# Ternary weights prepared beside the expert tiles, and attention rows gathered behind a batch's parts

## What is computed

```python
# layer 1 ffn: 8 experts, 2 for each token
topk_logits, selected = jax.lax.top_k(hidden_states @ Wr, 2)
p = jax.nn.softmax(topk_logits)
for e in range(8):
    w_e = jnp.where(selected == e, p, 0.0).sum(-1, keepdims=True)
    g = jnp.clip(silu(x @ Wg[e]), -7.0, 7.0)
    out = out + ((g * (x @ Wu[e])) @ Wd[e]) * w_e
# layer 2 attention: 8 heads a batch, 16 rows of 128 to a head
sm = softmax(einsum('bdm,bdn->bmn', qh, kh) * scale);  ret = einsum('bmn,bcn->bcm', sm, vh)
# layer 2 ffn: three matrices, each rounded to -1, 0, 1 by the mean of its absolute values
s = 1.0 / clip(mean(abs(w)), 1e-5);  qw = clip(round(w * s), -1, 1) / s
# layer 3 attention (16 heads a batch, masked), layer 3 ffn: three matrices, rounded the same way
q = clip(round(w / mean(abs(w))), -1, 1) * mean(abs(w))
```

## Time and profile before

| | us |
|---|---|
| median of the 3 runs (2516.19 to 2522.55) | 2522.51 |
| the profiled execution | 2525.09 |
| its span, first to last instruction | 2523.3 |
| MoeTop2 (1451.8 to 1629.5), its tile loop from about 1506 | 177.7 |
| Attention 2 (1629.6 to about 1843) | 213 |
| Attention 3 (2058 to about 2386) | 328 |

### The profile page before, as it was taken

How to read it: one execution, slowest core, us unless ns; L and a number is a source line. 1 busy time by engine, 2 the same in 40 slices (tenths; PEclk the granted TensorE clock), 3 DMA queues, 4 the chain that set the end, 5 groups by cost and what they waited for, 6 DMA issues and landing times. The chain is left out here.

```text
span 2523.3 us, 42640 instructions
## 1 busy us (share of the span) xinstructions
PE 2034.0 (81%) x13467; PEld 1242.7 (49%) x13467; DVE 1814.2 (72%) x4020; ACT 1403.7 (56%) x3553; POOL 1186.2 (47%) x1393
## 2 busy tenths in 40 slices
PE   5999698996799999999999849837835437887487
PEld 2444265663567776777777646514412223333144
DVE  4899485665799999999998663368837756888254
ACT  0777422451688888888888713215634423677343
POOL 3444102443788888888887523276312204333100
PEclk9999779998999999999999959958866656899699
DMA  4466313782300000000000042379610025576100
GB/s 133 138 188 171 100 48 106 249 260 82 59 16 20 20 22 16 20 20 22 16 16 3 1 151 88 117 188 237 174 47 1 0 87 133 153 198 159 44 1 34
DMA packets 256886, 223.20 MB, mean 88 GB/s; under 512 B 36441, under 2 KB 237756, under 8 KB 256028
## 3 DMA queue, kind: packets, MB, share of 16 engines
q1 hardware_dynamic: 231932, 173.06, 24.3%
q0 software_dynamic: 12240, 32.39, 5.1%
q10 hardware_dynamic: 12496, 15.03, 1.8%
HBM read 141.98 MB, written 79.32 MB: 88 GB/s over the span
## 5 line engine op out<-in xcount | busy, mean ns | idle before, releaser
L844 ACT ACTIVATE a_PT<-bank 128x512 f32<-128x512 f32 x640 | 355.8, 602 | 148.7 <-PE bank L607 132.3
L734 DVE TENSOR_REDUCE a_nm<-bank 128x2 f32<-128x512 f32 x640 | 409.2, 683 | 35.1 <-PE bank L600 32.9
L600 PE MATMUL bank<-a_stack_k,a_stack_q 48*128 48x256 bf16 (+2 forms) x1280 | 263.2, 298 | 108.9 <-DVE a_nm L734 75.3
L2913 PE MATMUL bank<-f_w,f_zc 128*128 128x512 bf16 x1152 | 283.9, 383 | 22.8 <-DVE f_zc L3021 18.2
L3233 POOL TENSOR_TENSOR f_hr<-f_hr,half_pow 128x4 f32<-128x4 f32 x192 | 244.5, 1273 | 84.8 <-DVE f_hr L3030 84.6
L607 PE MATMUL bank<-a_stack_q,a_stack_k 51*128 51x256 bf16 (+2 forms) x1280 | 252.2, 287 | 8.6 <-ACT a_PT L844 8.0
L600 PEld LDWEIGHTS bank<-a_stack_k,a_stack_q 48*128 48x128 bf16 (+2 forms) x1280 | 91.7, 99 | 272.9 <-DVE a_nm L734 195.8
L3125 ACT ACTIVATE f_Pm<-bank,f_nmax 128x128 f32<-128x128 f32 x512 | 182.5, 382 | 73.5 <-DVE f_nmax L3045 73.5
L622 PE MATMUL bank<-a_PT,a_V 128*32 128x256 f32 x2560 | 188.3, 416 | 1.4 <-ACT a_PT L844 1.4
L2913 PEld LDWEIGHTS bank<-f_w,f_zc 128*128 128x128 bf16 x1152 | 112.2, 99 | 123.0 <-issue 25.4
L3222 POOL TENSOR_TENSOR f_cf<-f_cbr,f_cmr 128x516 f32<-128x516 bf16 x128 | 157.0, 1226 | 12.6 <-DVE f_cb L3070 11.0
(11 more groups left out here) (370 smaller groups left out, 4721.2 us busy)
## 6 DMA issues: line engine op xcount, KB each, us to landing
cut<-a_parts SPq DMA_DIRECT2D x96, 192.0 KB
cut<-a_parts SPq DMA_DIRECT2D x144, 128.0 KB
o<-a_O SPq DMA_DIRECT2D x32, 512.0 KB
a_stack_q<-cut SPq DMA_DIRECT2D x64, 192.0 KB
a_stack_k<-cut SPq DMA_DIRECT2D x64, 192.0 KB
m_w<-in_w SPq DMA_DIRECT2D x32, 368.0 KB
moe_out<-m_oe ACTq DMA_DIRECT2D x32, 256.0 KB
a_num<-o SPq DMA_DIRECT2D x48, 128.0 KB
```

Of the source, the lines that this page charges most:

```text
L600: x = t.matmul(ps[:, n * D:(n + 1) * D], self.stack_q[rows, i, slot, n * P:(n + 1) * P], self.stack_k[rows, i, slot, :], start=True, stop= ...
L734: v.tensor_reduce(self.nm[:, g % 2, :, at % self.J, at // self.J], self.k.bank[h % 3][:, :].rearrange("p (n m) -> p n m", n=2), AX.X, ALU. ...
L844: a.activation(self.PT[:, h % 8, :, :].rearrange("p m n -> p (m n)"), self.k.bank[3 + h % 3][:, :], ACT.Exp).then_inc(self.a_exp.sem, 1)
L2913: x = t.matmul(ps[:, :], self.zc[:, b % 2, j, c_, :], self.fp8.w3[:, m, c_, at:at + BANK], start=(m == 0 and c_ == 0), stop=(m == 2 and c_ ...
```

## The change

1. The ternary weights of both layers leave the attentions. `MoeTop2` gets both `TernaryWeights`; the float copies and sums are allocated in its memory, the rounded bf16 matrices and the means in memory that lasts to the end. SP loads the matrices in 15 pieces of at most 768 columns (9 for layer 2, 6 for layer 3): six ahead of the first tile's store, three ahead of each of the next three stores. DVE sums in the tile steps 4 to 12, one piece behind `product` and one behind `copy_out`; PE adds over the partitions at step 13; DVE rounds from step 14 on, two instructions a step.
2. `pairs.gather(b + 2)` moves on POOL from offset 0 of batch b to its offset 15.
3. The eight PSUM banks become slices of one tensor; `two_banks` isn't called.

The core of the diff:

```diff
 class TernaryWeights:
     def allocate(self, ctx):
-        self.w = s("wf", [P, 3, self.width])
-        self.w16 = s("w16", [P, 3, self.width], BF16)
+        self.w16, self.m = s("w16", [P, 3, self.width], BF16), s("m", [P, 3])
+    def allocate_work(self, ctx):
+        self.w = s("wf", [P, 3, self.width])
-    def load(self, e):
+    def loads(self, e):
         for j, n in enumerate(self.names):
-            e.dma_start(self.w[:, j, :], self.k.A[n]).then_inc(self.d_w.sem, 16)
+            for at, size in self.pieces:
+                e.dma_start(self.w[:, j, at:at + size], self.k.A[n][:, at:at + size]).then_inc(self.d_w[j].sem, 16)
+                yield
 class Attention(Stage):
     def dve(self, v):
-            if 0 <= t < 60:
-                next(sums, None)
...
-            if t > 61:
-                next(steps, None)
     def act(self, a):
-        if self.ternary:
-            self.ternary.load(a)
     def pool(self, g):
                 if at < self.NV:
                     self.clear_V(g, at)
-                if self.pairs and at + 2 < B:
-                    self.pairs.gather(g, at + 2)
...
                 g.tensor_tensor(self.parts[:, i, :, 2, :], self.rest[:, i, :, :], self.parts[:, i, :, 1, :],
                                 ALU.subtract).then_inc(self.g_p2.sem, 1)
+            at = self.starts(t, 15)
+            if at is not None and self.pairs and at + 2 < B:
+                self.pairs.gather(g, at + 2)
 class MoeTop2(Stage):
+    TOTAL = 13
     def sp(self, sp):
         self.load_experts(sp, range(4, self.NE))
+        weights = chain.from_iterable(x.loads(sp) for x in self.ternaries)
         for j in range(self.NT):
+            for _ in range(3 if j else 6):
+                next(weights, None)
             sp.wait_ge(self.v_oe.sem, self.v_oe.at(j + 1))
     def pe(self, t):
+            if i == self.TOTAL + 2:
+                for x in self.ternaries:
+                    t.wait_ge(x.v_mean.sem, x.v_mean.at(1))
+            if i == self.TOTAL:
+                t.wait_ge(self.a_xT.sem, self.a_xT.at(i - 1))
+                for n, x in enumerate(self.ternaries):
+                    x.total(t, self.at_total(n))
     def dve(self, v):
                 self.product(v, i - 1)
+            if 4 <= i < self.TOTAL:
+                next(sums, None)
+            if i > self.TOTAL:
+                next(rounding, None)
             if i >= 3:
                 self.copy_out(v, i - 3)
+            if 4 <= i < self.TOTAL:
+                next(sums, None)
+            if i == self.TOTAL:
+                v.wait_ge(self.p_xT.sem, self.p_xT.at(i + 1))
+                for n, x in enumerate(self.ternaries):
+                    x.means(v, self.at_total(n))
+            if i > self.TOTAL:
+                next(rounding, None)
```

More of the change, by code:

```diff
@@ L1 @@
 from contextlib import ExitStack
+from itertools import chain
 import numpy as np
@@ L102, in __init__ @@
         self.sig = Signals(nc, ctx)
-        self.bank = [ctx.enter_context(nc.psum_tensor(f"bank{i}", [P, BANK], F32)) for i in range(8)]
+        self.psum = ctx.enter_context(nc.psum_tensor("bank", [P, 8 * BANK], F32))
+        self.bank = [self.psum[:, i * BANK:(i + 1) * BANK] for i in range(8)]
         self.X = self.sb("X", [P, B, D])
@@ L674, in dve @@
         self.dve_parameters(v)
-        sums = self.ternary.sums(v) if self.ternary else iter(())
-        steps = self.ternary.rounding(v) if self.ternary else iter(())
         for t in self.steps():
@@ L1982, in dve @@
         self.list_tokens(v)
+        sums = chain.from_iterable(x.sums(v) for x in self.ternaries)
+        rounding = chain.from_iterable(x.rounding(v) for x in self.ternaries)
         for i in range(self.NT + 3):
@@ L1989, in dve @@
                 self.places(v)
+            if 4 <= i < self.TOTAL:
[6 more added lines that the diff above has]
+                next(rounding, None)
+        for _ in rounding:
+            pass
     def moments(self, v, g):
@@ L3249, in program @@
         if 0 in stages:
-            stage(Attention(k, 0, None))
+            stage(Attention(k, 0))
         if 1 in stages:
@@ L3258, in program @@
         with ExitStack() as memory:
-            pairs = Pairs(k) if 3 in stages else None
-            if 3 in stages:
-                pairs.allocate(memory)
-                stage(MoeTop2(k, pairs))
+            pairs = Pairs(k)
+            l2.allocate(memory)
+            l3.allocate(memory)
+            with ExitStack() as rows:
+                pairs.allocate(rows)
+                if 3 in stages:
+                    stage(MoeTop2(k, pairs, (l2, l3)))
+                if 4 in stages:
+                    stage(Attention(k, 2, pairs))
             if 4 in stages:
-                l2.allocate(memory)
-                stage(Attention(k, 2, l2, pairs))
                 stage(Bitnet(k, l2))
-        if 6 in stages:
-            with ExitStack() as memory:
-                l3.allocate(memory)
-                stage(Attention(k, 3, l3))
+            if 6 in stages:
+                stage(Attention(k, 3))
                 stage(TernaryFfn(k, l3))
```

48 lines of the change are left out of this document (21 added, 27 removed).

## The result

The changed kernel takes 2600.6 us (median of 4, 2596.4 to 2603.6) against 2522.1 us before (2516.2 to 2522.6): 1.0316 times as long, interval 1.0292 to 1.0339, or +78.5 us. The forecast of 2601 us holds.

A forecast was written before the change was run, and what follows sets the result against it. No single engine was taken to bound the kernel; each stage has its own limit. Terms +93.8 - 5 - 11 + 1 = +78.8 us on 2525.1 gave 2603.9, stated as 2601 us against the runs' median, range 2562 to 2630.

The forecast's parts named there:

- The ring: Attention 2: moving the gather closes a loop of parts, gather, landing, add, moments and ACT's first part; +93.8 us.
- landing, among heads: Attention 2, later batches: time from the gather's second issue until its rows land, taken as 5.2 us, ends 2.8 and 6.6.
- moments to parts: fill, middle, heads: Attention 2: from DVE's moments to the end of ACT's first part, 2.3 us early, 4 between, 6.6 later with hand-over.
- rival 1: Attention 2: every gather lands in the shortest 2.8 us, turns of 12.0, 13.8 and 16.3 us; 2572 us, chance 0.22.
- The start: Attention 2: without 3 MB of weight loads batch 0's rows land sooner, so the chain starts 3.9 us earlier (0 to 3.9).
- MoeTop2: Tile loop taking over the weights' sums and roundings: PE could stall 0 to 3 us, taken as +1; no gain possible.
- Rival 4: MoeTop2's loop gives the gain back, costing +5 to +8 us instead of +1; 2607 us, sharing the forecast's chance of 0.54.
- Layer 3: Attention 3 without weights: 9.1 us of rounding and 2 us of sums go, -11 us (-9 to -14).
- The tail of Attention 2: Layer 2: ten rounding instructions behind batch 15's add go, 0.5 us each, -5 us (-2 to -7).
- PE's clock: Attention 2: pauses put PE at 1.2 GHz part of the time, granted clock nearer 0.6 than 0.71; link 6.5 us.
- 2 had 14.8, 17.6 and 20.7: Rival with a slower loop in Attention 2: landings 5.6 and 6.6 us, PE's clock low throughout; 2627 us, chance 0.16.
- Rival 3: Faster than before: the gather's wait in Attention 2 is hidden and the weights' move gains; 2493 us, chance 0.06.

The follow-up runs named there:

- The dose of 1.9 us a turn: Changed kernel with two of POOL's three instructions for the parts done twice in layer 2: 2631.1 us, 1.0431 of the kernel before.

## Why the prediction was right, point by point

**What waits for what** held, and it is what carried the forecast. The ring was put together from the order of the lists and from single links of the trace of before, and all of its links are in the trace of after, with nothing else between them. The two halves separately, +99.5 us on the adds for the gather and 31 us less time for the weights, settle it against the weights' move. The gather at the same place with one batch more of lead, 100 us faster, settles it against the place in POOL's list. The dose of 1.9 us a turn that came back 14 times shows that the turn is the sum of its links.

**The links**, as predicted and as measured in the changed kernel:

| link | predicted us | measured us |
|---|---|---|
| parts to second issue | 5.0 | 4.6; 5.3 in the last three turns |
| landing, fill | 4.3 | 4.6 to 5.4, mean 4.95 (batches 3 to 6) |
| landing, among heads | 5.2 | 3.7 to 5.3, mean 4.6 |
| add and moments | 1.9 | 1.87 |
| moments to parts: fill, middle, heads | 2.3, 4, 6.6 | 2.4, 3.8, 6.4 to 6.85 |
| four turns in the fill | 54 | 55.3 |
| two in the middle | 32.4 | 30.2 |
| seven among heads | 130.9 | 126.4 |

From the first issue (1635.08) to add 15 the changed kernel needs 231.9 us where 238.1 were predicted: 6 too many, most of it the landing among heads. The reason given for taking 5.2, traffic as before plus SP's stores of the same parts, left out that a ring at half the pace has less traffic (DMA share 0.54 against 0.92 in the earlier trace rows). How much each of the two does to the landing no run separates. All landings of the gathers in the ring, from a query of their line between 1640 and 1870 us; it counts both DMAs of a pair, each from its own issue, where the table counts from the second issue to the add:

```profile
DMA to landing us min/median/max: 3.1/3.7/5.4
```

None is as short as rival 1 wanted throughout (2.8 us; two turns with 2.9 were seen in the kernel with the gather ahead of the parts). The term for parts to second issue was too long by 0.4 us in eleven turns. The estimate of 2.3 us by the Trainium skill ("DMA: Bandwidth & Descriptors", "Anatomy of one DMA") is under every landing measured here; the measurement decides. A link wasn't in the forecast: POOL's addition into X, 0.7 us, which from batch 13 on stands between parts and gather.

**The start.** First issue to first add 7.94 us before, 4.10 after: 3.84 sooner, as the 3.9 predicted. The stage itself began 3.4 us later, so add 0 stands where it stood. That the weights' loads were the reason is borne out by the kernel with the gather alone, which still has them: 8.26 us.

**MoeTop2**, predicted +1. DVE's timeline in a turn with two sums:

```profile
1522.96 0.29 DVE L2179 TENSOR_SCALAR n_sg<-n_sg 128x256 f32<-128x256 f32 x1 [1.87 <-ACT n_sg L2232]
...
1523.70 0.95 DVE L263 TENSOR_REDUCE w_gate_sums<-w_gate_wf 128x1 f32<-128x768 f32 x1
...
1524.89 0.94 DVE L263 TENSOR_REDUCE w_gate_sums<-w_gate_wf 128x1 f32<-128x768 f32 x1
1525.98 0.29 DVE L2179 TENSOR_SCALAR n_sg<-n_sg 128x256 f32<-128x256 f32 x1
```

The turn stays at 3.02 us and the idle time of 1.87 us is used up. (A sum takes 0.86 us here; the rows that the prediction cites give 0.85, which changes nothing.) PE is busy for all of 18 us and all of 40 us in two windows of the loop at granted clock 1.00, and its two matmuls with the totals cost some 0.4 us. The stage began 1.9 us later than in the trace of before and ended 3.4 later; the difference, 1.5, is near the 1 predicted, and 1.1 of it lies ahead of the first tile, where none of this work is. From the loop's first clamp to its last it is 112.8 and 112.7 us in the two kernels with the weights in the attentions and 113.2 to 113.6 in the ten traces with them here: the loop pays 0.4 to 0.9 us. Rival 4 (the loop gives the gain back) isn't seen.

**Layer 3**, predicted -11: from Bitnet's first moments to TernaryFfn's 498.1 us, before 510.2: -12.1. SP's first store of each batch's parts in Attention 3 tells where. In the kernel before, the batches 2 to 4:

```profile
2104.03 0.38 SPq L520 DMA_DIRECT2D cut<-a_parts  x1
2124.94 0.38 SPq L520 DMA_DIRECT2D cut<-a_parts  x1
2141.52 0.41 SPq L520 DMA_DIRECT2D cut<-a_parts  x1
```

and in the changed kernel the batches 2 to 7:

```profile
2193.63 0.38 SPq L526 DMA_DIRECT2D cut<-a_parts  x1
2210.20 0.39 SPq L526 DMA_DIRECT2D cut<-a_parts  x1
2227.01 0.41 SPq L526 DMA_DIRECT2D cut<-a_parts  x1
2241.07 0.41 SPq L526 DMA_DIRECT2D cut<-a_parts  x1
2256.03 0.51 SPq L526 DMA_DIRECT2D cut<-a_parts  x1
2270.57 0.51 SPq L526 DMA_DIRECT2D cut<-a_parts  x1
```

The turns of 19.7 and 18.0 us, to the batches 6 and 7, are now 15.0 and 14.5: -8.2 where -9.1 was put. The turn to batch 3, behind the six sums, fell from 20.9 to 16.6: -4.3 where -2 was put, inside its bounds of 0 and 5.2. So the term is there with both its parts. "14.3 us a batch through" was too smooth all the same: the turns to the batches 3 and 4 take 16.6 and 16.8 us with nothing rounded beside them, and the second took 16.6 before.

**The tail of Attention 2**, predicted -5 for ten roundings behind add 15: add 15 to Bitnet's first moments took 86.8 us before and 85.4 after, -1.4. This term failed in size. The ten roundings are there behind the add of batch 15, and they cost what was put, but only for a while: the ninth maximum behind that add comes 13.0 us after it before and 11.6 with the gather alone, against 7.9 to 10.2 in all kernels without the weights' work (8.3 in the changed kernel, 4.7 sooner). At the 24th maximum it is 26.4 and 25.5 against 23.3 to 25.6 (24.4 in the changed kernel), so most of the delay is gone by then. The step that failed is to take the delay as lasting to the end of the stage; what sets the pace of the last heads isn't shown. Down to Bitnet's first moments the kernels without the work scatter from 81.7 to 86.6 us, and the kernel with the gather alone has 84.2; what is left of the term is no larger than this scatter. (Attention 2 before ends later than the about 1843 us given above: the last addition into X starts at 1855.45. And TernaryFfn's first moments stand at 2372.9, so Attention 3 ends ahead of that and not at about 2386.)

**The sum.** Against the prediction: the stages ahead of MoeTop2 +1.9, MoeTop2 +0.5, the ring -6.1, the tail +3.6, layer 3 -1.1, TernaryFfn +0.7: -0.5 in all. That the time was hit to half a microsecond is luck: an error of 6 us and one of 4 had opposite signs, and the 1.9 us ahead of MoeTop2 are within the scatter of that position. What the prediction earned is the mechanism, and the size of the ring to within 7% (6.1 of 93.8 us).

**PE's clock.** 0.57 and 0.52 in the first two windows, 0.66 among heads: between the two numbers given (0.6 and 0.71), not clearly nearer the lower. The link of 6.4 to 6.85 us lies between the 6.0 and 7.1 read at clock 1.00 and 0.66. The mean of a whole turn hides what the link itself ran at. The link of the turn shown above, and the same link with the ring open (gather put back, the second run), columns as in the earlier trace rows:

```profile
1794.81:1801.65 6.84, 6.18 (x36) 3.06 (x37) 4.52 (x9) 2.62 (x6) 0.58 (x1) 0.50 0.60 145
```

```profile
1717.58:1722.48 4.90, 4.24 (x42) 2.54 (x42) 4.86 (x10) 2.71 (x7) 3.50 (x8) 1.00 1.13 302
```

In the seven links among heads the granted clock is 0.50 to 0.67, and PE is busy for all but some 0.7 us of each. With the ring open the link takes 4.9 us in five turns of that run, all at clock 1.00. So a ring that leaves PE idle for half of each turn meets the lower level of 1.2 GHz in the link where PE is needed. The seven links are 6.7 us on the mean; how much of the 1.8 us is the clock and how much the order of the work no run separates.

**Rivals.** 1 had turns of 12.0, 13.8 and 16.3, 2 had 14.8, 17.6 and 20.7; measured were 13.8, 15.1 and 18.05, between them. Rival 3's 2493 us is the time of the version with the gather put back: its price for the weights' part was right, its condition, a hidden wait, was not met in the changed kernel.

**A faster version.** The weights' move with the gather left where it was takes 2490.6 to 2494.7 us and beats both kernels, by 1.2% and 4.2%.

## What to carry to other kernels

When a transfer is moved closer to its use, follow the user's results back to the issuer: if what is ahead of the issue in its list waits for something behind the use, the distance in steps is no longer a lead but a ring, and each batch pays the full sum of issue, landing and links. Such a ring shows as many half-idle engines, each released by its neighbour, and it can be priced ahead of time link by link; room found on an engine inside it is no room, and one batch more of lead removes it at the same place in the list. Before filling an idle time, look at what ended each part of it: here 25 of 27 us lay ahead of a barrier.

## What the runs showed that was not expected

- DVE's add, 128x256 f32, takes 0.48 us in every batch of the ring, where POOL is idle beside it; with the ring open it takes 0.47 to 1.81 (mean 0.85 before, 0.71 with the gather put back), where POOL is at work beside it. The shorter adds gain nothing there, since DVE waits for the rows anyway.
- The landing of the same gather depends on when it is issued: from the second issue to the add 2.9 us in the first turns of the kernel with the gather ahead of the parts, 7.0 to 7.6 in its last ones, 3.6 to 5.5 for nearly all behind the parts. The traffic differs between these kernels as well, so the moment isn't shown to be the reason.
- On POOL an indirect DMA behind the clearing begins after an idle time of 0.58 us, where it is 0.17 behind the parts (first issue of a pair).
- PE's granted clock was 0.94 to 0.97 among heads (1707 to 1761 us) in the three runs with the ring open and the parts as they were (gather put back, twice, and V cleared first), near its higher level of 2.4 GHz, and 0.66 in the closed ring, where PE waits for DVE's maxima in every turn.
